# Delta heads of a decoder layer: the lower triangle made in mid-slot and stored whole, the decays one slot ahead

## The chip, the cores and the metric

The kernel runs on one core of a Trainium2 chip. The metric is the device time of one execution in microseconds; runs are compared by their medians. Engines are named PE or TensorE (matrix products), DVE or VectorE, ACT or ScalarE, POOL or GpSimd, and SP or SyncE, which here only issues DMAs.

## The reference

One decoder layer on x of shape (4, 512, 512), in float32: a gated delta rule with 16 heads of 128, then cross attention, then self attention and a mixture of experts. The change touches the delta heads only:

```python
q, k, v = conv_silu(x @ Wq.T), conv_silu(x @ Wk.T), conv_silu(x @ Wv.T)   # causal, 4 taps
g = exp(-exp(A_log) * softplus(a + dt_bias)); beta = sigmoid(b)
q, k = l2norm(q), l2norm(k)            # x / max(sqrt(sum x^2), 1e-12)
def step(S, (q_t, k_t, v_t, g_t, beta_t)):
    error = v_t - g_t * (S . k_t)
    S = g_t * S + k_t x (beta_t * error)
    return S, S . q_t
o = rmsnorm(o) * norm_w * silu(x @ Wg.T);  return o @ Wo.T
```

## The kernel before

**Chunks.** The recurrence is computed in chunks of 128 tokens, CH = 4 chunks (c = 0 to 3) in each of 16 heads, all four sequences of the batch at once (tiles of 128 x 4 x 128). Per chunk: `D` is the exponential of sums of log decays; `Lo` is the strictly lower triangle of k k^T times D and scales; the inverse of I + Lo (`W`, and `T` turned) gives `U` from `R` (v less what S retrieves); `PT` (q k^T times decays, turned) times U, plus `oi` (S times q), gives the output `o`; and S is updated with `Kd` and U.

**Slots.** `slot(i, c, ...)` is written out once for each engine, and each engine runs its list strictly in order; semaphores join the lists. The slot of chunk n merges the inverse and applies it for chunk n, makes q, v, the gate, P and Kd for chunk n+1, and k, the decays D and Lo for chunk n+2. The flags back, has1, has2 leave out what lies outside the range. The loop over heads holds the four slots of a head; the last head stands behind it.

**The inverse.** The sixteen-wide diagonal blocks of Lo (eight for each of four sequences) are inverted by GpSimd, on 32 partitions, in `solve`: a mask (L930), a diagonal (L932), 14 pairs of a product (L937) and a subtraction (L940), and a turned copy `W16` (L942). How they travel is SP's list: `diagonal_blocks` waits for `lo_ready` and stores the eight blocks with eight DMAs; `fetch_blocks` brings them to `L16` with 32 partitions; `spread` stores T16 and W16 into two zeroed images in DRAM and fetches the whole images as `T` and `W`. TensorE then merges blocks of 16 to 32, 64, 128: `spread_rows(l)` (W and Lo), `merge(l)` (Y and T), `turn_inverse(l)`; `spread_rows(0)` is a slot's first work and waits for `tw_in`.

**Order around the change.** In a slot of before, TensorE runs: spread_rows(0), half of k's projection, S k, merge(0), the other half, v turned, turn_inverse(0), spread_rows(1), q's projection around merge(1), turn_inverse(1), spread_rows(2), S q (for oi), v's projection around merge(2), the product for U, k k^T (kk), q turned, the products for o and S, the decay products (L635, L636), q k^T, k turned, the gate's projection, P turned, o turned. In c = 1 and c = 2 the raw weights of the next head are turned just ahead of the last step, and in c = 3 at two earlier places; ScalarE rounds them to `w_lead`, DVE makes `w_rest`. A projection is 12 products of 512 columns (L506). DVE's list has, late in the slot: the v taps, the squares of k (diag, its sum), o, S, P, Kd, then for both norms at once a maximum and a reciprocal of ScalarE's square root (L886), the scales `once` and `twice`, and Lo. GpSimd's list: Sd (S times a decay), in c = 2 and 3 a copy of a row of head constants, `lgm` (two products, the decay products' right side, L966), the solve, the halos of k, q and v (the last three tokens, carried to the next chunk), Dm (D cut to the triangle), grq and end, and the sum osq. A halo waits for ScalarE's copy of the projection (`copy_pre`, L820 and L821).

Of the kernel before, what the change touches and what calls it, by code (L numbers as in the profile page):

```python
# [5 lines left out]
ALU = mybir.AluOpType  # L6
# [6 lines left out]
P = 128  # L13
# [300 lines left out]
def delta_heads(nc, xn_parts, A, const_dram, ptab, osq, og_dram, blocks_dram, images_dram):  # L314
# [10 lines left out]
    with ExitStack() as ctx:  # L325
        sem = semaphores(nc, ctx, "gd")

        def sb(n, s, d=F32):
# [19 lines left out]
        root = sb("root", [P, 2, B])  # L348
        rn = sb("rn", [P, 2, 2, B])
# [25 lines left out]
        none = sb("none", [P, B, 4])  # L375
        L16 = sb("L16", [BK, SB, SB])
# [21 lines left out]
        kdiag, k_len, q_len, root_done, max_done, rnorm_done, once_ready, scales_done, extra_done = (  # L398
            sem(x) for x in ("kdiag", "klen", "qlen", "root", "max", "rnorm", "once", "scales", "extra"))
# [13 lines left out]
        def slots(eng, slot):  # L413

            slot(-1, 2, False, False, True, True)
            slot(-1, 3, False, True, True, True)
            with eng.Fori(0, LAST) as i:
                for c in range(CH):  # L420
                    slot(i, c, True, True, True, True)
            for c in range(CH):
                slot(LAST, c, True, c < CH - 1, c < CH - 2, False)

        @block.sync
        def _(sp):
# [4 lines left out]
            def diagonal_blocks(m, par):  # L431
                sp.wait_ge(lo_ready, m + 1)
                for k in range(P // SB):
                    rows = slice(k * SB, (k + 1) * SB)
                    sp.dma_start(blocks_dram[par, :, k].rearrange("b i j -> i b j"), Lo[rows, par, :, rows]).then_inc(lo_out, 16)

            def fetch_blocks(m, par, back):
                sp.wait_ge(lo_out, (m + 1) * 16 * (P // SB))
                if back:
                    sp.wait_ge(solved, m)  # L440
                sp.dma_start(L16[:].rearrange("p i j -> p (i j)"), blocks_dram[par].rearrange("b k i j -> (b k) (i j)")).then_inc(l16_in, 16)

            def spread(m, par):
                sp.wait_ge(solved, m + 1)
                for image, small in zip(images_dram, (T16, W16)):
# [4 lines left out]
                for image, whole in zip(images_dram, (T, W)):  # L450
# [7 lines left out]
            def slot(i, c, back, has1, has2, more):  # L458
# [3 lines left out]
                if has2:  # L462
                    diagonal_blocks(n + 2, c % 2)
# [28 lines left out]
        def _(pe):  # L492
# [31 lines left out]
            def slot(i, c, back, has1, has2, more):  # L524
# [63 lines left out]
                if back:  # L588
                    turn_inverse(1)
                    spread_rows(2)  # L590
# [22 lines left out]
                if has2:  # L613
                    pe.wait_ge(k_silu, n + 3)
                    if has1:
                        pe.wait_ge(lo_ready, n + 2)
                    each(Bk[4], k_c, k_c, kk_done)
                if has1:
# [3 lines left out]
                    turned(Bk[5], q_m, q_turned)  # L622
                if back:
# [7 lines left out]
                if has2:  # L631
                    pe.wait_ge(lgm_ready, n + 3)
                    if has1:
                        pe.wait_ge(d_exp, n + 2)
# [3 lines left out]
                if has1:  # L638
                    each(Bk[3], q_m, k_m, qk_done)
# [7 lines left out]
                if back and more and c in (1, 2):  # L647
                    pe.wait_ge(v_pre, n + 4)
                    turn_weights(i + 1, JK if c == 1 else JV)
                if back:  # L650
                    pe.wait_ge(o_ready, n + 2)
                    if has2:
                        pe.wait_ge(d_exp, n + 3)
# [11 lines left out]
        def _(dve):  # L665
# [14 lines left out]
            def slot(i, c, back, has1, has2, more):  # L680
# [45 lines left out]
                if back:  # L726
                    inverse_rows(1)
                    masked(2)
                if has1:
# [5 lines left out]
                if has1:  # L735
                    tap(n + 1, parm, PQ, cur_a, (2,), q_tap)
                    dve.wait_ge(v_halo, n + 2)
                    dve.wait_ge(v_pre, n + 4)
                    tap(n + 1, parm, PV, cur_a, (0, 1, 2), v_tap)
                if back and more and c == CH - 1:  # L740
                    rest_weights(h1, JG)
                if has2:
                    dve.wait_ge(kk_done, n + 3)
                    nc.vector.tensor_tensor(diag[:], Bk[4][:, :, :], ident.unsqueeze(1).to_broadcast([P, B, P]), ALU.mult).then_inc(kdiag, 1)
                    dve.wait_ge(kdiag, n + 3)
                    nc.vector.tensor_reduce(root[:, 0, :], diag[:], AX.X, ALU.add).then_inc(k_len, 1)
                if back:
                    dve.wait_ge(o_sum, n + 1)
                    dve.wait_ge(o2_ready, n + 1)
                    if c > 0:  # L750
                        for b in range(B):
                            st = nc.vector.scalar_tensor_tensor(out=o[:, b, :], in0=Bk[2][:, b, :], scalar=rn[:, par, 1, b:b + 1],
                                                                in1=oi[:, b, :], op0=ALU.mult, op1=ALU.add)
                        st.then_inc(o_ready, 1)
                    else:
                        nc.vector.tensor_tensor(o[:], Bk[2][:, :, :], bc(rn[:, par, 1, :], P), ALU.mult).then_inc(o_ready, 1)
                    dve.wait_ge(s_sum, n + 1)
                    if c > 0:
# [2043 lines left out]
```

## Time and profile before

| | us |
|---|---|
| median of 3 runs | 4028.65 |
| lowest, highest | 4025.49, 4032.96 |
| profiled execution, own time | 4027.95 |
| its span | 4026.1 |

| engine | busy us | share of the span |
|---|---|---|
| PE | 3447.7 | 86% |
| PE weight loads | 2733.0 | 68% |
| DVE | 2154.6 | 54% |
| ACT | 1774.1 | 44% |
| POOL | 1503.7 | 37% |

The page divides the span into 40 slices of 100 us. From the second to the twentieth PE is at nine tenths or more, and these are the delta heads (101 to some 1993 us); behind them come the other stages, which the change does not touch. A wait is read from the idle time just before an instruction, with what released it. Start times below are in microseconds from the start of the span. Matrix products of 128 by 128 in float32 stand twice for each product, so four sequences give x8.

### The profile page before, as it was taken

The numbers are of one execution on the slowest core, as the hardware profiler recorded it, in microseconds if no ns is written. First come the engines' busy times: TensorE is split into PE (matmuls) and PEld (weight loads), VectorE is DVE, ScalarE is ACT, GpSimd is POOL, SyncE is SP. The second block draws the span as 40 slices with busy tenths as digits, with TensorE's granted clock in tenths as the row PEclk, the third lists the DMA queues.
The fourth block names the chain that finished last, engine by engine and source line by source line (L and its number), as shares of the span: only waits on it lengthen the run. The fifth ranks groups of instructions, "written<-read, shape, count | busy, mean of one in ns | idle before, by whom it ended". The sixth has DMA issues, their size and how long they took to land. (4 is left out here: it accounts for less than half of the span.)

```text
span 4026.1 us, 62497 instructions
## 1 busy us (share of the span) xinstructions
PE 3447.7 (86%) x19682; PEld 2733.0 (68%) x19682; DVE 2154.6 (54%) x4501; ACT 1774.1 (44%) x4509; POOL 1503.7 (37%) x2924
## 2 busy tenths in 40 slices
PE   3799999999999999999799488869979999974993
PEld 1688888888888888888677244458856666654441
DVE  2566666666666666666432577745536546532223
ACT  2456555555655555556421155534434434431110
POOL 2466665656666666666300100045532000003203
PEclk9899999999999999999899699989989999985996
DMA  2111111111111111111243400023344120115324
GB/s 65 36 48 38 34 41 44 40 44 41 44 41 33 41 39 45 44 41 28 85 120 119 165 11 13 13 66 108 120 158 154 53 83 31 52 63 203 126 91 154
DMA packets 399009, 279.41 MB, mean 69 GB/s; under 512 B 137520, under 2 KB 323760, under 8 KB 397776
## 3 DMA queue, kind: packets, MB, share of 16 engines
q1 hardware_dynamic: 391504, 257.42, 21.2%
q0 software_dynamic: 5120, 16.78, 1.3%
q10 hardware_dynamic: 2304, 4.20, 0.3%
q8 instruction: 43, 0.70, 0.1%
q14 instruction: 38, 0.31, 0.0%
HBM read 179.22 MB, written 99.09 MB: 69 GB/s over the span
## 5 line engine op out<-in xcount | busy, mean ns | idle before, releaser
L506 PE MATMUL gd_PJ<-xn_lead,gd_w_rest 128*128 128x512 f32 x1024 | 449.6, 439 | 17.6 <-DVE gd_w_rest L669 17.6
L506 PE MATMUL gd_PJ<-xn_lead,gd_w_lead 128*128 128x512 f32 x1024 | 411.7, 402 | 0.0
L506 PE MATMUL gd_PJ<-xn_rest,gd_w_lead 128*128 128x512 f32 x1024 | 409.2, 400 | 0.0
L676 DVE SCALAR_TENSOR_TENSOR gd_conv<-gd_pre,gd_cur_a,gd_conv 128x512 f32<-128x512 f32 x384 | 298.1, 776 | 154.6 <-ACT gd_conv L821 147.5
L940 POOL TENSOR_TENSOR gd_T<-gd_T,gd_prod 32x14 f32<-32x14 f32 (+6 forms) x896 | 328.4, 366 | 70.2
L937 POOL TENSOR_TENSOR gd_prod<-gd_L,gd_T 32x14 f32<-32x14 f32 (+6 forms) x896 | 316.5, 353 | 70.2
L516 PE MATMUL gd_B<-gd_W,gd_Lo 128*128 128x64 f32 x1536 | 210.2, 283 | 95.5 <-DMA gd_W<-turned_image 95.5
L820 ACT COPY gd_pre<-gd_PJ 128x512 f32<-128x512 f32 x192 | 111.3, 580 | 380.3 <-PE gd_PJ L506 379.5
L516 PEld LDWEIGHTS gd_B<-gd_W,gd_Lo 128*128 128x128 f32 x1536 | 199.8, 203 | 103.3 <-DMA gd_W<-turned_image 89.7
L506 PEld LDWEIGHTS gd_PJ<-xn_lead,gd_w_rest 128*128 128x128 f32 x1024 | 199.0, 194 | 47.6 <-DVE gd_w_rest L669 21.8
L506 PEld LDWEIGHTS gd_PJ<-xn_lead,gd_w_lead 128*128 128x128 f32 x1024 | 197.3, 193 | 45.9
L506 PEld LDWEIGHTS gd_PJ<-xn_rest,gd_w_lead 128*128 128x128 f32 x1024 | 199.3, 195 | 27.0
L516 PEld LDWEIGHTS gd_B<-gd_Y,gd_T 128*128 128x128 f32 x1536 | 195.7, 192 | 25.6 <-DVE gd_Y L689 11.9
L2475 POOL MEMSET ms_rank<- 128x1 f32 x8 | 0.3, 98 | 561.4 <-POOLq L55 561.4
L2185 PE MATMUL sa_B<-sa_kT,sa_qT 128*128 128x512 f32 (+3 forms) x512 | 181.3, 478 | 29.7 <-DMA sa_qT<-turned_queries_keys 17.6
L695 DVE TENSOR_TENSOR gd_W<-gd_W,gd_B 128x256 f32<-128x256 f32 x192 | 80.6, 420 | 227.1 <-PE gd_B L516 227.0
L516 PE MATMUL gd_B<-gd_Y,gd_T 128*128 128x64 f32 x1536 | 195.7, 270 | 5.5 <-DVE gd_Y L689 5.5
L2249 ACT ACTIVATE sa_E<-sa_B,sa_nmax 128x512 f32<-128x512 f32 (+3 forms) x256 | 132.2, 524 | 152.4 <-DVE sa_nmax L2299 152.4
L2235 PE MATMUL sa_B<-sa_wo_lead,sa_o_parts 128*128 128x512 f32 x512 | 163.3, 400 | 8.8 <-issue 8.8
L1830 PE MATMUL sp_B<-sp_w_lead,sp_h_rest 128*128 128x512 f32 x384 | 157.6, 410 | 11.3 <-POOL sp_h_rest L1961 11.3
L1422 POOL TENSOR_TENSOR xt_xt<-x_xres,x_bpb 128x512 f32<-128x512 f32 x16 | 20.4, 1279 | 366.1 <-DVE xt_y L1638 305.3
L676 DVE SCALAR_TENSOR_TENSOR gd_conv<-gd_pre,gd_cur_k,gd_conv 128x512 f32<-128x512 f32 x192 | 153.4, 799 | 6.6 <-ACT gd_conv L821 4.3
(400 smaller groups left out, 8842.3 us busy)
## 6 DMA issues: line engine op xcount, KB each, us to landing
turned_queries_keys<-f_wq SPq DMA_DIRECT2D x16, 1280.0 KB, 6.0
gd_T<-inverse_image SPq DMA_DIRECT2D x64, 256.0 KB, 2.9
gd_W<-turned_image SPq DMA_DIRECT2D x64, 256.0 KB, 3.3
gated_outputs<-gd_og SPq DMA_DIRECT2D x64, 256.0 KB, 2.6
go_ogt<-gated_outputs SPq DMA_DIRECT2D x16, 1024.0 KB, 6.8
sa_qT<-turned_queries_keys SPq DMA_DIRECT2D x16, 1024.0 KB, 5.6
gathered<-sa_blank SPq DMA_DIRECT2D x39, 256.0 KB, 7.2
ms_xr<-gathered SPq DMA_DIRECT2D x39, 256.0 KB, 2.7
```

The costliest lines, as they stand in the source:

```text
L506: mm = pe.matmul(bank, w_parts[wp][:, j, k, :], rhs, start=(k == 0 and wp == 1), stop=(k == KT - 1 and wp + xp == 0))
L516: mm = pe.matmul(bank[:, b, :], lhs[b], rhs[b], start=True, stop=True)
L676: nc.vector.scalar_tensor_tensor(out=conv[:, j], in0=pre[:, parm, j, :, d:d + P], scalar=cur[:, 4 * j + d:4 * j + d + 1], in1=conv[:, j], ...
L695: nc.vector.tensor_tensor(second(W_c, s), second(W_c, s), half[3].rearrange("p b (g m) -> p b g m", m=s), ALU.add).then_inc(w_ready, 1)
L820: nc.scalar.copy(pre[:, parm, j, :, 3:3 + P], bank)
L937: nc.gpsimd.tensor_tensor(prod[:, rows, 0:j], L16[:, rows, j:j + 1].to_broadcast(shape), T16[:, j:j + 1, 0:j].to_broadcast(shape), ALU.mul ...
L940: nc.gpsimd.tensor_tensor(T16[:, rows, 0:j], T16[:, rows, 0:j], prod[:, rows, 0:j], ALU.subtract).then_inc(solving, 1)
L1422: nc.gpsimd.tensor_tensor(xt[:, par, :], xres[:, bass.ds(t, 1), :].rearrange("p o d -> p (o d)"), bpb[:, :], ALU.add).then_inc(bias_ready, 1)
L1830: mm = pe.matmul(bank[:, :], h_parts[hp][:, s, k, :], w_parts[wp][:, k, j, :], start=(k == 0 and hp == 1), stop=(k == KT - 1 and hp + wp = ...
L2185: pe.matmul(Bk[bank][:, col:col + w], qT[:, h, i * P:(i + 1) * P], kT[:, h // REP, 0:w], start=True, stop=False)
L2235: mm = pe.matmul(Bk[i][:, :], part(o_parts, h, op)[:, i * P:(i + 1) * P], wo_parts[wp][:, h, :], start=(h == 0 and op == 1), stop=(h == HE ...
L2249: ex = nc.scalar.activation(E[:, par, E_AT[i]:E_AT[i] + w], Bk[bank][:, col:col + w], ACT.Exp, bias=nmax[:, par, i:i + 1], accum_out=sums[ ...
```

## The change

- **Lo in mid-slot.** TensorE computes kk ahead of spread_rows(2). DVE forms the diagonal's product ahead of masked(2) and its sum (`kss`) behind it. ScalarE takes the square root of kss alone (`klen`), behind the oi copies and ahead of q's SiLU. DVE then makes the maximum, the reciprocal (`krn`), once, twice and Lo between q's last tap and the v taps.
- **q's norm.** ScalarE sums q's squares into `qss`; DVE takes the maximum with 1e-24; GpSimd raises it to -0.5 (`qrn`), ahead of grq.
- **Whole triangle stored once.** SP stores all of Lo (256 KB) with one DMA, and fetch_blocks picks the diagonal blocks out of DRAM with a stride. In spread, W goes ahead of T.
- **Decays one slot ahead.** A further flag has3: lgm, the decay products, Exp and Dm's source belong to chunk n+3. lgm now reads the table `ptab`, and stands on GpSimd behind the halos. A slot (-1, 1) is added at the start.
- **Others.** q k^T stands behind q's turning, ahead of the product for o. On ScalarE, U is copied ahead of v's projection. In c = 1 and 2 the raw weights are turned ahead of the decay products, rounded ahead of Exp, and w_rest stands behind S. GpSimd's solve stands first in its slot, with the row copy behind its first instruction, and Sd behind it.

ScalarE, slot c = 1, from the oi copies to the square of q; before:

```order
L854 ACTIVATE gd_oi<-gd_B1,gd_grq 128x128 x4
L825 ACTIVATE gd_qT<-gd_conv 128x512
L820 COPY gd_pre<-gd_PJ 128x4x128
L821 ACTIVATE gd_conv<-gd_PJ,gd_cur_a 128x512
L863 COPY gd_U<-gd_B1 128x512
L870 ACTIVATE gd_osqr,gd_root<-gd_B5 128x128 x4
```

And in the changed kernel:

```order
L867 ACTIVATE gd_oi<-gd_B1,gd_grq 128x128 x4
L871 ACT_TABLE_LOAD
L871 ACTIVATE gd_klen<-gd_kss 128x4
L838 ACT_TABLE_LOAD
L838 ACTIVATE gd_qT<-gd_conv 128x512
L877 COPY gd_U<-gd_B1 128x512
L833 COPY gd_pre<-gd_PJ 128x4x128
L834 ACTIVATE gd_conv<-gd_PJ,gd_cur_a 128x512
L888 ACTIVATE gd_osqr,gd_qss<-gd_B5 128x128 x4
```

The square root with two table loads has come between the oi copies and q's SiLU, and U's copy stands ahead of v's.

TensorE, slot c = 1, from the product for U to k's turning; before (B4 holds kk, B3 q k^T, B0 the decay sums):

```order
L516 MATMUL gd_B1<-gd_R,gd_W 128x128 x4
L516 MATMUL gd_B4<-gd_kT 128x128 x4
L521 MATMUL gd_B5<-gd_cst,gd_qT 128x128 x4
L516 MATMUL gd_B2<-gd_U,gd_PT 128x128 x4
L516 MATMUL gd_B1<-gd_U,gd_Kd 128x128 x4
L635 MATMUL gd_B0<-gd_lgm_rest,gd_upr 128x512
L636 MATMUL gd_B0<-gd_lgm_lead,gd_upr 128x512
L516 MATMUL gd_B3<-gd_kT,gd_qT 128x128 x4
L521 MATMUL gd_B5<-gd_cst,gd_kT 128x128 x4
```

And in the changed kernel, the same place:

```order
L521 MATMUL gd_B1<-gd_R,gd_W 128x128 x4
L526 MATMUL gd_B5<-gd_cst,gd_qT 128x128 x4
L521 MATMUL gd_B3<-gd_kT,gd_qT 128x128 x4
L521 MATMUL gd_B2<-gd_U,gd_PT 128x128 x4
L521 MATMUL gd_B1<-gd_U,gd_Kd 128x128 x4
L641 REGISTER_ALU
L502 MATMUL gd_PJ<-gd_cst,gd_wraw 128x128 x4
L647 MATMUL gd_B0<-gd_lgm_rest,gd_upr 128x512
L648 MATMUL gd_B0<-gd_lgm_lead,gd_upr 128x512
```

kk has left this place (it stands ahead of spread_rows(2)), q k^T has moved up, and the weights are turned ahead of the decay products.

GpSimd, from the end of one slot to the solve of the next (osq to T16), before:

```order
L991 TENSOR_TENSOR osq<-osq,gd_o2 128x4
L957 TENSOR_TENSOR gd_Sd<-gd_S,gd_end 128x512
L966 TENSOR_TENSOR gd_lgm_lead<-gd_cur_k,gd_cst 128x512
L966 TENSOR_TENSOR gd_lgm_rest<-gd_cur_k,gd_cst 128x512
L927 ISA
L929 REGISTER_ALU
L930 TENSOR_TENSOR gd_T16<-gd_L16,gd_below 32x256
```

And in the changed kernel, from the solve's last instruction in c = 1 to the end of the slot:

```order
L952 TENSOR_TENSOR gd_W16<-gd_T16,gd_blank 32x256
L977 TENSOR_TENSOR gd_Sd<-gd_S,gd_end 128x512
...
L992 TENSOR_TENSOR gd_lgm_lead<-ptab,gd_cst 128x512
...
L992 TENSOR_TENSOR gd_lgm_rest<-ptab,gd_cst 128x512
L998 TENSOR_TENSOR gd_Dm<-gd_D,gd_tril 128x512
L1001 TENSOR_TENSOR gd_qrn<-gd_qss,gd_minus_half 128x4
L1003 TENSOR_TENSOR gd_grq<-gd_cur_a,gd_qrn 128x4
L1004 COPY gd_end<-gd_cur_a 128x4
L1008 TENSOR_TENSOR osq<-osq,gd_o2 128x4
```

Sd and lgm have gone from ahead of the solve to behind it.

The diff, cut to its core:

```diff
-            def diagonal_blocks(m, par):
+            def store_triangle(m, par):
                 sp.wait_ge(lo_ready, m + 1)
-                for k in range(P // SB):
-                    rows = slice(k * SB, (k + 1) * SB)
-                    sp.dma_start(blocks_dram[par, :, k].rearrange("b i j -> i b j"), Lo[rows, par, :, rows]).then_inc(lo_out, 16)
+                sp.dma_start(lo_dram[par, :, 0:P, :].rearrange("b t s -> t b s"), Lo[:, par]).then_inc(lo_out, 16)
 ...
+                a = lo_dram[par]
+                src = bass.AP(tensor=a.tensor, offset=a.offset, ap=[[SB * P + SB, BK], [P, SB], [1, SB]])
+                sp.dma_start(L16[:], src).then_inc(l16_in, 16)
 ...
                     turn_inverse(1)
+                if has2:
+                    pe.wait_ge(k_silu, n + 3)
+                    if has1:
+                        pe.wait_ge(lo_ready, n + 2)
+                    each(Bk[4], k_c, k_c, kk_done)
+                if back:
                     spread_rows(2)
 ...
                     turned(Bk[5], q_m, q_turned)
+                    if back:
+                        pe.wait_ge(pt_ready, n + 1)
+                    each(Bk[3], q_m, k_m, qk_done)
 ...
+                if has3:
+                    pe.wait_ge(lgm_ready, n + 4)
+                    if has2:
+                        pe.wait_ge(d_exp, n + 3)
 ...
+                if has2:
+                    act.wait_ge(k_len, n + 3)
+                    nc.scalar.activation(klen[:, :], kss[:, :], ACT.Sqrt).then_inc(k_root, 1)
                 if has1:
                     act.wait_ge(q_tap, (n + 2) * 3)
                     silu(PQ, qT[:, parm, :], q_silu)
-                    act.wait_ge(v_proj, n + 2)
-                    copy_pre(parm, PV, JV, cur_a, v_pre)
 ...
                     pool.wait_ge(v_pre, n + 4)
+                    if has2:
+                        pool.wait_ge(darg, n + 3)
                     halo(parm, c1, PV, v_halo)
+                if has3:
+                    for part, col in zip(lgm, (P_LG, P_LGR)):
+                        at = col + c3 * B
+                        lg = ptab[:, bass.ds(h3, 1), at:at + B].rearrange("p o n -> p (o n)")
+                        tt = nc.gpsimd.tensor_tensor(part[:], bc(lg, P), later.unsqueeze(1).to_broadcast([P, B, P]), ALU.mult)
+                    tt.then_inc(lgm_ready, 1)
 ...
+                    pool.wait_ge(q_max, n + 2)
+                    nc.gpsimd.tensor_tensor(qrn[:, parm, :], qss[:, :], minus_half[:], ALU.pow).then_inc(q_rnorm, 1)
```

## Rows read from the trace of the kernel before

**Rows 1.** Busy time by stage, 14 heads: length, PE, PEld, DVE, ACT, POOL, clock, DMA.
```profile
293.37:1917.67 1624.30, 1526.62 (x10192) 1372.12 (x10192) 1019.31 (x2142) 919.83 (x2296) 1012.29 (x2311) 0.97 0.16 40
```

**Rows 2.** Waits of PE, 200 to 1800 us: total us, times, longest.
```profile
PE gd_B L516 <- DMA gd_W<-turned_image: 69.7, 28, 4.5
```

**Rows 3.** PE in order of time, starts of slots: start, us, instruction, [idle before <-releaser].
```profile
1018.99 1.00 PE L516 MATMUL gd_B<-gd_W,gd_Lo 128*128 128x64 f32 x8
1020.77 0.50 PE L506 MATMUL gd_PJ<-xn_lead,gd_w_rest 128*128 128x512 f32 x1 [0.78 <-DVE gd_w_rest L669]
...
1022.27 1.05 PE L516 MATMUL gd_B<-gd_S,gd_kT 128*128 128x128 f32 x8
...
1047.77 1.10 PE L516 MATMUL gd_B<-gd_W,gd_Lo 128*128 128x64 f32 x8 [1.00 <-DMA gd_W<-turned_image]
...
1105.42 1.97 PE L516 MATMUL gd_B<-gd_W,gd_Lo 128*128 128x64 f32 x8 [3.92 <-DMA gd_W<-turned_image]
...
1109.86 1.73 PE L516 MATMUL gd_B<-gd_S,gd_kT 128*128 128x128 f32 x8
```

**Rows 4.** Busy time in a stretch behind the long wait; the clock is third from last.
```profile
1106.00:1108.00 2.00, 2.00 (x9) 1.90 (x9) 0.42 (x1) 0.00 (x0) 0.77 (x1) 0.50 0.07 6
```

**Rows 5.** SP and POOL in order of time: slots c=1 (first two rows) and c=2.
```profile
993.68 0.72 POOL L930 TENSOR_TENSOR gd_T<-gd_L,gd_below 32x256 f32<-32x256 f32 x1 [3.00 <-DMA gd_L<-diagonal_blocks]
...
1006.75 0.84 POOL L942 TENSOR_TENSOR gd_W<-gd_T,gd_blank 32x256 f32<-32x256 f32 x1
...
1019.17 3.60 SPq L435 DMA_DIRECT2D diagonal_blocks<-gd_Lo  x8
...
1021.30 0.20 POOL L991 TENSOR_TENSOR osq<-osq,gd_o 128x4 f32<-128x4 f32 x1 [3.34 <-ACT gd_osqr L898]
...
1025.61 0.72 POOL L930 TENSOR_TENSOR gd_T<-gd_L,gd_below 32x256 f32<-32x256 f32 x1 [0.66 <-DMA gd_L<-diagonal_blocks]
...
1040.73 0.84 POOL L942 TENSOR_TENSOR gd_W<-gd_T,gd_blank 32x256 f32<-32x256 f32 x1
...
1044.28 0.51 SPq L451 DMA_DIRECT2D gd_W<-turned_image  x1
```

**Rows 6.** PE in order of time, middle of slot c=1.
```profile
1003.68 1.00 PE L516 MATMUL gd_B<-gd_W,gd_Lo 128*128 128x64 f32 x8
1004.52 1.11 PE L516 MATMUL gd_B<-gd_S,gd_qT 128*128 128x128 f32 x8
...
1009.15 1.05 PE L516 MATMUL gd_B<-gd_R,gd_W 128*128 128x128 f32 x8
...
1010.93 0.60 PE L521 MATMUL gd_B<-gd_cst,gd_qT 128*128 128x128 f32 x4
...
1013.07 0.48 PE L635 MATMUL gd_B<-gd_lgm_rest,gd_upr 128*128 128x512 f32 x1
```

**Rows 7.** ACT in order of time, middle of slot c=1.
```profile
1003.12 0.64 ACT L825 ACTIVATE gd_kT<-gd_conv 128x512 f32<-128x512 f32 x1 [2.81 <-DVE gd_conv L676]
...
1005.67 1.14 ACT L854 ACTIVATE gd_oi<-gd_B,gd_grq 128x128 f32<-128x128 f32 x4 [0.76 <-PE gd_B L516]
1008.34 0.63 ACT L825 ACTIVATE gd_qT<-gd_conv 128x512 f32<-128x512 f32 x1 [1.53 <-DVE gd_conv L676]
1009.35 0.59 ACT L820 COPY gd_pre<-gd_PJ 128x512 f32<-128x512 f32 x1 [0.37 <-PE gd_PJ L506]
1009.83 0.78 ACT L821 ACTIVATE gd_conv<-gd_PJ,gd_cur_a 128x512 f32<-128x512 f32 x1
```

**Rows 8.** ACT, the table loads around the square root in slot c=1.
```profile
1015.62 1.28 ACT L886 ACT_TABLE_LOAD   x1
1016.91 0.21 ACT L886 ACTIVATE gd_root<-gd_root 128x8 f32<-128x8 f32 x1
1017.14 1.28 ACT L889 ACT_TABLE_LOAD   x1
```

**Rows 9.** Groups of POOL instructions, whole run: busy us, mean ns, idle before.
```profile
L966 POOL TENSOR_TENSOR gd_lgm_rest<-gd_cur_k,gd_cst 128x512 fp32r<-128x512 f32 x64 | 66.5, 1040 | 0.0
```

More of the change, by code:

```diff
@@ L522, in turned, with slot @@
                 tr.then_inc(done, 1)
-            def slot(i, c, back, has1, has2, more):
+            def slot(i, c, back, has1, has2, has3, more):
                 n = i * CH + c
@@ L678, in tap, with slot @@
                                                    op0=ALU.mult, op1=ALU.add).then_inc(done, 1)
-            def slot(i, c, back, has1, has2, more):
+            def slot(i, c, back, has1, has2, has3, more):
                 n = i * CH + c
@@ L736, in slot @@
                     tap(n + 1, parm, PQ, cur_a, (2,), q_tap)
[L737 to L741, printed above, removed]
-                if has2:
[L743 to L758, printed above, removed]
-                        dve.wait_ge(sd_ready, i * (CH - 1) + c)
-                        nc.vector.tensor_tensor(S[:], Bk[1][:, :, :], Sd[:], ALU.add).then_inc(s_ready, 1)
-                    else:
-                        nc.vector.tensor_copy(S[:], Bk[1][:, :, :]).then_inc(s_ready, 1)
@@ L825, in silu, with slot @@
                 nc.scalar.activation(dst, conv[:, j].rearrange("p b t -> p (b t)"), ACT.Silu).then_inc(done, 1)
-            def slot(i, c, back, has1, has2, more):
+            def slot(i, c, back, has1, has2, has3, more):
                 n = i * CH + c
@@ L891, in slot @@
                     nc.scalar.copy(PT[:], Bk[3][:, :, :]).then_inc(pt_ready, 1)
-                if back and more and c in (1, 2):
-                    lead_weights(i + 1, JK if c == 1 else JV)
                 if back:
@@ L942, in solve, with slot @@
                 nc.gpsimd.tensor_tensor(W16[:], T16[:].rearrange("p i j -> p j i"), blank[:], ALU.add).then_inc(solved, 1)
-            def slot(i, c, back, has1, has2, more):
+            def slot(i, c, back, has1, has2, has3, more):
                 n = i * CH + c
@@ L957, in slot @@
                     nc.gpsimd.tensor_tensor(Sd[:], S[:], bc(end[:, par, :], P), ALU.mult).then_inc(sd_ready, 1)
-                if has1 and c == CH - 1:
-                    row(cur_a, h1, head_a)
-                if has2:
-                    if c == 2:
-                        row(cur_k, h2, head_k)
-                    if has1:
-                        pool.wait_ge(darg, n + 2)
-                    for part, col in zip(lgm, (P_LG, P_LGR)):
-                        tt = nc.gpsimd.tensor_tensor(part[:], bc(cur_k[:, col + c2 * B:col + c2 * B + B], P),
-                                                     later.unsqueeze(1).to_broadcast([P, B, P]), ALU.mult)
-                    tt.then_inc(lgm_ready, 1)
-                if has1:
-                    solve(n + 1, back)
                 if has2:
```

179 lines of the change are left out of this document (107 added, 72 removed).

## The prediction

> **What bounds the kernel now.** I read in this order: busy time by stage, what TensorE waits for, one head in order of time, then the chain behind the longest wait. In the steady part of the delta stage TensorE is busy 1526.62 of 1624.30 us, at a mean granted clock of 0.97 [rows 1]. No other engine comes near, so the stage lasts as long as TensorE's work, plus its idle time, plus what a lowered clock costs. The idle time has one large cause: the first products of a slot, which need W and T from their images in DRAM. Fourteen heads hold 28 such waits, 69.7 us in all [rows 2], two in each head of four slots. In the head shown they are 1.00 us at 1047.77 (start of slot c=3) and 3.92 us at 1105.42 (start of c=1) [rows 3]. [...] From the slot's first products to those of S and k it is 4.44 us (1105.42 to 1109.86); after a start at full clock it is 3.28 with 0.78 of waiting in it (1018.99 to 1022.27), so 2.50. The products of S and k then take 1.73 instead of 1.05 [rows 3]. That is 1.94 + 0.68 = 2.6 us per head. The third item is the 0.78 us for w_rest at 1020.77 [rows 3].
>
> **Why the images are late.** In slot c=2 Lo is stored from 1019.17 by eight DMAs that take 3.60 us to issue; GpSimd, free since 1021.50, does its other work and begins the solve when the blocks have landed, at 1025.61; W16 is done at 1041.57, the last image fetch is issued at 1044.28, and TensorE starts at 1047.77 [rows 3, 5]. From the start of the solve to TensorE's start it is 22.2 us, in a slot of 28.8.
>
> **What the change takes away.** Lo no longer comes at the end of DVE's slot but in its middle, so it is stored, fetched and waiting before the next slot begins. Now GpSimd's own end of slot starts the solve: the osq addition, over at 1021.50, against 1025.61, 4.1 us earlier [rows 5]. The 2.1 us of lgm and 1.04 of Sd stand behind the solve. The solve may get shorter too: it took 13.9 us in c=1 (993.68 to 1007.59) and 15.96 in c=2 (1025.61 to 1041.57) [rows 5]. DVE's v taps begin when ScalarE has scaled v, 1010.61 in c=1 [rows 7], 8.4 before the next slot and after the solve; the same point of c=2 is 1038.4, inside it. Started earlier, the solve ends ahead of the v taps in every slot. The chain of 22.2 us from 2.5 us after the slot's start gives images at about 24.7 at the latest, against a slot of 26.5 to 28. So I take both waits as gone: 31 of them (28, and 3 more outside the window read) at 69.7 / 28 = 2.49 is 77 us; the clock with them, 15 x 2.6 = 39; and 15 of the 0.78 waits, 12, since the raw weights are now turned ahead of the decay products and rounded ahead of Exp. **Removed: 128 us.** The store grows from eight pieces of 4 KB to one of 256 KB; the nearest rows are the image fetches of that size, of which TensorE saw the last landed 3.5 us after issue (1044.28 to 1047.77) [rows 3, 5]. Before, Lo was stored 2.05 us after the root's end (1017.12 to 1019.17) [rows 5, 8]; with the root ending at 3.8 on the scale below, Lo is ready at about 5.9, over 8 us before the slot's end at 14.5, so this is covered.
>
> **What it puts in the way.** Time zero is the start of the S and q products, 1004.52, in slot c=1; the PE and ScalarE rows of that slot give the rest [rows 6, 7].
> - *The key products (kk)* now stand ahead of the products at 1003.68. They need kT, whose SiLU ends at 1003.76. So TensorE waits where it did not: 0.15 to 0.2 us in each of some 62 slots, **12 us**. Their own 0.89 us (half of 1009.15 to 1010.93) is only moved.
> - *The square root in mid-slot.* ScalarE's oi copies end at 2.29. Then a table load of 1.28, the root 0.21, a table load of 1.28 [rows 8], and qT's SiLU of 0.63: done at 5.75, against 4.45 before. TensorE reaches the turning of q at 5.52 (u products at 4.63 plus 0.89), where it had kk as cover before. It waits 0.3 us. In the 47 slots with c > 0: **14 us**. (In c = 0 there is no oi, the loads run early and nothing waits.)
> - *The decays one slot ahead.* lgm now stands on GpSimd behind the halo of v, which waits for v's projection on ScalarE. ScalarE: qT to 5.75, U (a copy of 0.59) to 6.25 with the usual overlap, v's copy and scaling (1009.35 to 1010.61, 1.26) to 7.4 [rows 7]. GpSimd: halo 0.2 (as the osq addition [rows 5]), two lgm products of 1.04 [rows 9]: ready at 9.7 to 9.8. TensorE: q turned at 5.8, then the turning, o and s products (1010.93 to 1013.07, 2.14) and the moved query-key products, 0.89, to 8.83, a weight turning of 0.36 (2.14 less two times 0.89), 9.2 [rows 6]. It waits 0.5 us. Before, lgm was made at the slot's start and nothing waited for it. In c = 0, u to v ready is 1.06 + 0.59 + 1.16 = 2.8, lgm at 5.1 after u's start, while TensorE is there at 0.89 + 2.14 + 0.89 = 3.9: 1.2 us. Sum 47 x 0.5 + 15 x 1.2 = **42 us**.
>
> The two small edits have one answer: the two square roots that were one become a ScalarE root for k and a power on GpSimd for q, off the path, since the power comes some 2 us ahead of the osq addition for which GpSimd waits anyway; no row shows a power, and the nearest, additions on 128x4 such as osq's, take 0.20 [rows 5]. Moving the query-key products earlier gives U's copy its cover back and costs nothing.
>
> **Sum.** New waits 12 + 14 + 42 = 68; 128 - 68 = 60. Filling and draining the pipeline has the same chain twice (eight stores become one, 3.60 us of issue [rows 5]); I take 5 us. The profiled execution took 4027.95 us (span 4026.1), near the median of 4028.65. **Forecast: 4027.95 - 65 = 3963 us.** Bounds of each unknown: the new waits are 0 at least (every one sits on 0.2 to 1.2 us of estimated edge) and could be 110 if each chain is 0.7 us slower than put together here, since they add up directly: 3895 to 4005.
>
> [...] The rows say that a switch of table costs its 1.28 us and nothing else: the root at 1016.91 follows the load begun at 1015.62 by 0.01 us, and the next load begins 0.02 after the root ends (1016.91 + 0.21 to 1017.14) [rows 8]. [...]
>
> **Rivals.**
> - *The new waits hardly show.* TensorE arrives later than I reckon, or the chains overlap more; then only the removal counts with a third of the new waits: 4027.95 - 128 + 22 - 5 = 3917, at the extreme 3895. For it: all three new waits are small against the rows they come from. Against: each follows from rows of one slot, and the slots repeat. Chance 0.17.
> - *The images stay late.* The changed blocks fetch and the whole-triangle store are not in the rows; if the blocks land after GpSimd is free, the solve starts no earlier. If half of the 77 + 39 us stays, 4027.95 - 128 + 58 + 68 - 5 = 4021, with new waits then partly hidden behind the stall, about 4005. Against it: Lo is ready some 8 us before the slot's end and needs about 3.5 + 3.5. Chance 0.10.
> - *ScalarE's mid-slot chain becomes the bound: slower.* The chain oi, root, qT, U, v, halo, lgm has no slack in my sum, so each microsecond more costs one per slot, 62 us. It decides from 65 / 62 = 1.05 us: beyond that the kernel is slower. [...] For it: three engines hand over in turn, and I count each hand-over as next to nothing. Against it: the rows with loads show no such gap. Chance 0.07. [...]
> - *GpSimd becomes the bound.* Solve, Sd, halos and lgm now stand in one line ahead of TensorE's decay products. From 2.5 after the slot's start: solve 14.5, Sd 1.04, halos and a row copy 0.8, so free at about 19. Zero above is 14.5 us before the next slot's first products (1004.52 to 1018.99) [rows 3, 6], so about 13.3 into a slot of 27.8, and v is ready at 13.3 + 7.4, nearly 21: 2 us of slack. A solve that stays at 16 still fits; a power that overruns all slack by 3 us would give 3963 + 3 x 62 = 4149. Chance 0.04, and 0.04 more for a small overrun that ends within 0.2%.
>
> **How the numbers follow.** Forecast case, 3935 to 3995: 0.58. The rivals have 0.17, 0.10, 0.07 and 0.08. The range takes in the forecast case, most of the first two rivals and the bounds above: 3900 to 4010. A difference of 0.2% (8 us) is about what can be told from none. Faster: 0.58 + 0.17 + most of the second rival, 0.84; within 0.2%: 0.06; slower: 0.10.
>
> **What would show it.** Right: no wait of TensorE for W's image in the steady slots; a mean clock of 0.99 or 1.00 there; the osq addition directly ahead of the solve; waits of TensorE for lgm of about 0.5 us (1.2 in c = 0), for qT about 0.3, for kT about 0.2; a table load of 1.28 after the oi copies; heads of about 112 us instead of 116. Wrong: image waits that remain; a wait of GpSimd for the blocks ahead of the solve; waits for lgm that end with GpSimd's products long after v is ready (GpSimd late), or waits for qT over 1 us (the chain on ScalarE).

## The result and the profile after

The changed kernel takes 4043.32 us (median of 6 runs, 4039.44 to 4045.72), the kernel before 4029.52 (median of 6): a ratio of 1.0035, 95% interval 1.0022 to 1.0048. The forecast of 3963 us and its range of 3900 to 4010 were wrong, and so was the sign. The profiled execution of after has a span of 4037.6 us.

A head of four slots is read off the copies of gd_cur_a on GpSimd, one per head: before 116.02 us on the mean of 14 heads, after 117.69 ((1889.77 - 242.11) / 14). The steady stretch of after, beside [rows 1], and all waits of TensorE from 200 to 1800 us, beside [rows 2]:

```profile
299.63:1942.95 1643.32, 1538.27 (x10195) 1359.79 (x10193) 1165.99 (x2198) 985.31 (x2351) 1076.33 (x2366) 0.98 0.18 48
```
```profile
PE gd_B L647 <- POOL gd_lgm_rest L992: 90.9, 55, 3.5
PE gd_PJ L511 <- DVE gd_w_rest L677: 5.7, 14, 0.4
PE gd_B L526 <- ACT gd_qT L838: 4.1, 26, 0.2
PE gd_B L521 <- ACT gd_kT L838: 0.3, 1, 0.3
```

The image waits (69.7 us there) are gone, and 90.9 us of waiting for the decay products lgm stand in their place; the clock rose only from 0.97 to 0.98. DVE is busy for 1165.99 us in 14 heads instead of 1019.31, with almost the same work (2198 instructions instead of 2142, the 56 more of them small). In order of time, one slot with c > 0 (c = 1), the three engines around that wait:

```profile
1026.96 0.22 POOL L931 TENSOR_TENSOR gd_pre<-gd_pre,gd_none 128x12 f32<-128x12 f32 x1 [3.97 <-ACT gd_conv L834]
1027.13 1.49 POOL L992 TENSOR_TENSOR gd_lgm_lead<-ptab,gd_cst 128x512 fp32r<-128x512 f32 x1
1028.58 1.49 POOL L992 TENSOR_TENSOR gd_lgm_rest<-ptab,gd_cst 128x512 fp32r<-128x512 f32 x1
```
```profile
1026.92 3.70 DVE L684 SCALAR_TENSOR_TENSOR gd_conv<-gd_pre,gd_cur_a,gd_conv 128x512 f32<-128x512 f32 x3 [0.52 <-ACT gd_conv L834]
```
```profile
1028.43 0.60 PE L502 MATMUL gd_PJ<-gd_cst,gd_wraw 128*128 128x128 f32 x4
1030.12 0.50 PE L647 MATMUL gd_B<-gd_lgm_rest,gd_upr 128*128 128x512 f32 x1 [1.09 <-POOL gd_lgm_rest L992]
```

v's scaled copy releases GpSimd's halo and DVE's three v taps at the same moment. They run side by side and both are slow: a product takes 1.49 us instead of 1.04 [rows 9], the three taps 3.70. TensorE waits 1.1 us, in c = 1, 2 and 3. In c = 0 it waits 3.50, and the cause lies earlier:

```profile
1095.71 0.20 POOL L1008 TENSOR_TENSOR osq<-osq,gd_o 128x4 f32<-128x4 f32 x1 [1.80 <-ACT gd_osqr L909]
1099.48 0.72 POOL L937 TENSOR_TENSOR gd_T<-gd_L,gd_below 32x256 f32<-32x256 f32 x1 [3.57 <-issue]
...
1115.06 1.03 POOL L992 TENSOR_TENSOR gd_lgm_lead<-ptab,gd_cst 128x512 fp32r<-128x512 f32 x1
1116.06 1.03 POOL L992 TENSOR_TENSOR gd_lgm_rest<-ptab,gd_cst 128x512 fp32r<-128x512 f32 x1
```
```profile
1117.14 0.71 PE L647 MATMUL gd_B<-gd_lgm_rest,gd_upr 128*128 128x512 f32 x1 [3.50 <-POOL gd_lgm_rest L992]
```
```profile
1118.00:1120.00 2.00, 2.00 (x8) 1.73 (x7) 2.00 (x4) 1.07 (x2) 0.32 (x1) 0.50 0.92 269
```

GpSimd has nothing to wait for ("issue") and still stands for 3.57 us at the first instruction of its loop body, in each of the 14 turns back to the loop's start (3.3 to 4.2 us). The last head stands behind the loop and has no such gap: its solve starts 0.02 us after osq, its wait for lgm in c = 0 is 1.92 us and the slot takes 26.9 instead of 30.1 to 31.2. In the loop the solve and everything behind it come that much later, and the clock behind TensorE's stall is 0.50, as it was behind the image wait [rows 4]. DVE is caught too: its v taps now begin while GpSimd is still at the late solve, and the last of the three takes 4.95 us instead of 0.75 (6.53 for the three), in the same 14 turns:

```profile
1112.35 6.53 DVE L684 SCALAR_TENSOR_TENSOR gd_conv<-gd_pre,gd_cur_a,gd_conv 128x512 f32<-128x512 f32 x3 [0.85 <-ACT gd_conv L834]
```

It ends at 1118.88, 0.55 us after GpSimd's row of W16, three halos, lgm and Dm (1113.25 to 1118.33). TensorE does not wait for it there, being late itself.

The page has one more hint, the queue for instructions (packets, MB, share), before and after:

```profile
q14 instruction: 38, 0.31, 0.0%
```
```profile
q14 instruction: 108, 0.88, 0.1%
```

Seventy more packets of 8 KB are five for each of the 14 times that the loop goes back to its start. GpSimd's compiled program of after has 67072 bytes for 1048 instructions, 64 bytes each, so a packet of 8192 bytes holds 128. The loop is instructions 159 to 493 from the start of that program (the trace leaves out the first 26). In the trace the five packets of a turn begin when GpSimd has come to numbers 160, 164 to 166, 225 to 229, 353 and 476.

### The profile page after: what moved, and what is told of

It reads as the page before. It is cut to its first block and busy times, and to the rows that moved or that the text cites. A ratio compares the mean times of both kernels' runs of the same rounds, so it can differ in the third digit from the quotient of the medians.

```text
span 4037.6 us, 62353 instructions
## 1 busy us (share of the span) xinstructions
PE 3452.8 (86%) x19651; PEld 2714.7 (67%) x19682; DVE 2312.6 (57%) x4563; ACT 1845.2 (46%) x4568; POOL 1580.2 (39%) x2989
## 5 line engine op out<-in xcount | busy, mean ns | idle before, releaser
L684 DVE SCALAR_TENSOR_TENSOR gd_conv<-gd_pre,gd_cur_a,gd_conv 128x512 f32<-128x512 f32 x384 | 457.3, 1191 | 46.2 <-ACT gd_conv L834 39.3
L950 POOL TENSOR_TENSOR gd_T<-gd_T,gd_prod 32x14 f32<-32x14 f32 (+6 forms) x896 | 305.9, 341 | 70.2
L947 POOL TENSOR_TENSOR gd_prod<-gd_L,gd_T 32x14 f32<-32x14 f32 (+6 forms) x896 | 278.7, 311 | 70.7
L521 PE MATMUL gd_B<-gd_W,gd_Lo 128*128 128x64 f32 x1536 | 192.6, 268 | 0.0
L521 PEld LDWEIGHTS gd_B<-gd_W,gd_Lo 128*128 128x128 f32 x1536 | 186.7, 192 | 0.0
```

The costliest lines, as they stand in the source:

```text
L521: mm = pe.matmul(bank[:, b, :], lhs[b], rhs[b], start=True, stop=True)
L684: nc.vector.scalar_tensor_tensor(out=conv[:, j], in0=pre[:, parm, j, :, d:d + P], scalar=cur[:, 4 * j + d:4 * j + d + 1], in1=conv[:, j], ...
L947: nc.gpsimd.tensor_tensor(prod[:, rows, 0:j], L16[:, rows, j:j + 1].to_broadcast(shape), T16[:, j:j + 1, 0:j].to_broadcast(shape), ALU.mul ...
L950: nc.gpsimd.tensor_tensor(T16[:, rows, 0:j], T16[:, rows, 0:j], prod[:, rows, 0:j], ALU.subtract).then_inc(solving, 1)
```

## The experiments

Theory A: lgm is late because of its place. Theory B: GpSimd fetches its own code again in every head. "Head" is measured as above.

| kernel | median us | ratio to before, interval | head | code packets |
|---|---|---|---|---|
| e1_lgm_first | 4035.11 | 1.0022, 1.0012 to 1.0032 | 117.38 | 108 |
| e2_short | 4047.03 | 1.0047, 1.0031 to 1.0064 | 117.77 | 38 |
| e3_first_short | 3953.44 | 0.9817, 0.9800 to 0.9833 | 111.31 | 38 |
| e4_before_padded | 4029.61 | 1.0001, 0.9992 to 1.0011 | 116.09 | 108 |
| e5_after_shifted | 4013.20 | 0.9964, 0.9950 to 0.9978 | 115.29 | 39 |
| e6_first_shifted | 3955.59 | 0.9813, 0.9797 to 0.9830 | 111.73 | 39 |
| e7_short_misplaced | 4032.37 | 1.0005, 0.9994 to 1.0015 | 117.07 | 109 |
| e8_pm_early | 3945.00 | 0.9788, 0.9772 to 0.9804 | 110.98 | 38 |
| e9_decay_first | 3918.08 | 0.9729, 0.9714 to 0.9743 | 109.31 | 38 |
| e10_squares_first | 3915.80 | 0.9714, 0.9700 to 0.9728 | 108.80 | 38 |
| e11_between_halos | 4109.06 | 1.0194, 1.0173 to 1.0214 | 121.76 | 39 |

### The products first: e1_lgm_first

```diff
+                if has3:
+                    if has2:
+                        pool.wait_ge(darg, n + 3)
+                    for part, col in zip(lgm, (P_LG, P_LGR)):
...
                     start_solve(n + 1, back)
...
                     pool.wait_ge(v_pre, n + 4)
-                    if has2:
-                        pool.wait_ge(darg, n + 3)
                     halo(parm, c1, PV, v_halo)
-                if has3:
-                    for part, col in zip(lgm, (P_LG, P_LGR)):
```

> The changed kernel with one move: on GpSimd the two decay products (lgm) and their wait for the last decay argument stand at the head of the slot, ahead of the first instruction of the solve, where before they stood behind the v halo. Two theories on the new loss. Theory A (place): the products come late because they stand behind the v halo, and each takes 1.49 us because DVE's v taps run beside them. It expects the TensorE wait for lgm_rest gone in c = 1, 2, 3 (1.09 to 1.11 us each now), the products near 1.04 us, three v taps back from 3.70 to near 2.4 us. Theory B (code): the 3.57 us in which GpSimd sits at the top of every head with nothing to wait for is its own code being loaded again; this kernel's loop is as long, so B expects that gap to stay near 3.5 us, but no longer in front of lgm: it then delays the solve of c = 0 by 3.5 + 2.1 us, and the images of the next slot come some 2 to 3 us late. With both: heads of 117.2 - 3 x 1.1 - 3.5 - 1 (half clock) + 3 = 112 to 113 us, time 3965 to 3985 us. With A alone and no gap: 109.5 us a head, 3925 us. If the place doesn't matter: 4040 us.

The lgm waits are gone and a product takes 1.04 us, as A says. Of the taps A is right in c = 0 alone, where three take 2.39 us; in c = 1 and c = 2 they take 3.28 and 3.76, now beside Dm, where they took 3.70. The gap stays, 45.7 us in 14 heads, as B says, and now delays the whole solve of c = 0. TensorE's next slot:

```profile
1114.31 0.63 PE L526 MATMUL gd_B<-gd_cst,gd_o 128*128 128x128 f32 x4 [1.89 <-ACT gd_D L899]
1116.61 1.10 PE L521 MATMUL gd_B<-gd_W,gd_Lo 128*128 128x64 f32 x8 [1.68 <-DMA gd_T<-inverse_image]
```
```profile
1118.00:1120.00 2.00, 2.00 (x6) 1.56 (x5) 0.18 (x1) 0.00 (x0) 2.00 (x3) 0.50 0.62 146
```

The place was worth 8 us only (forecast 60 to 80). The late images and the half clock are back: with the wait in front of it that slot (c = 1) is 31.0 to 32.8 us long here, against 28.6 in after. And where nothing is late on GpSimd, the 1.1 us of waiting for lgm were mostly cover for something else: in c = 2 TensorE now waits 0.90 us for Pm (the masked query-key product on DVE), in c = 3 1.25 for ScalarE's squares of q, and these slots are only 0.25 and 0.17 us shorter.

### A shorter loop: e2_short and e3_first_short

```diff
-                    halo(parm, c1, PQ, q_halo)
                     pool.wait_ge(v_pre, n + 4)
-                    halo(parm, c1, PV, v_halo)
+                    halo(parm, c1, PQ, v_halo)
...
-                        tt = nc.gpsimd.tensor_tensor(part[:], bc(lg, P), later.unsqueeze(1).to_broadcast([P, B, P]), ALU.mult)
+                    nc.gpsimd.tensor_tensor(lgm_both[:], two.unsqueeze(3).to_broadcast(whole),
+                                            later.unsqueeze(1).unsqueeze(1).to_broadcast(whole), ALU.mult).then_inc(lgm_ready, 1)
```

> The changed kernel with its order kept and GpSimd's loop body made shorter: the q and v halos are one instruction (behind q's and v's pre), and the two decay products are one instruction over both tables (128x1024 where there were two of 128x512). GpSimd's program then has 15 instructions less in the loop of four slots, about as many as the kernel before the change has. Theory B (GpSimd's loop does not fit what it holds of its code and is fetched again in every head): the 3.57 us gap at the top of the head goes to about 0.2 us, the instruction packets of the small queue go from 108 back to about 40, lgm is waited for about 1.1 us in c = 0 as in the other slots instead of 3.5 us, and the half clock behind it goes: 15 x (2.4 + 1.0) = 51 us less, 3985 to 3995 us. Rival C (the gap is the four weight loads, which SP now issues at that moment, or anything else of the order): nothing changes, 4035 to 4045 us with the gap in place. In c = 1, 2, 3 both expect the wait for lgm to stay at 1.1 us, since place and overlap are the same.

> Both edits: the decay product at the head of GpSimd's slot, and the short loop body. If A and B are both right no TensorE wait for lgm is left, no gap and no late image: 15 x (4 x 1.1 + 2.4 + 1.0) = 117 us less than the changed kernel, 3920 to 3935 us, heads of 109.4 us, clock 0.99 to 1.00. If only A holds (the gap stays): as the kernel with the move alone. If only B holds: as the kernel with the short body alone.

With the short loop the packets are 38, the gap is 4.2 us in 13 heads instead of 46.8, and c = 0 takes 27.1 us instead of 30.1 to 31.2. But the time doesn't fall. Theory B had 3985 to 3995 us; rival C had about the time that came, but with the gap still in place, and the gap is gone. Slots c = 1 and c = 2 grew from 28.6 to 29.4: TensorE's wait for lgm is half as long (0.55), but one product of 1024 beside the v taps stretches these from 3.70 to 4.83 us, and Pm, which stands behind them on DVE, is 1.15 late. Slot c = 3 grew most, from 29.9 to 31.1 and in every second head 32.7: behind the same taps the rest of the gate weights is 1.0 late, and in those heads the clock is 0.50 behind that wait. So e2 confirms B for c = 0 and hides it by a change of its own, which is why e5 below takes the reload away in another way. With both edits it is 3953 us: no wait for lgm, a gap of 0.4 us, no image wait; the head is 6.4 us shorter, though either edit alone gave nothing (0.3 and -0.1). That is 90 us of the 117 expected. What is left are waits that the sum of the expectation did not have, for Pm (19.5 us from 200 to 1800) and for the squares of q (17.4).

### Length or place of the loop: e4, e5, e6, e7

Each adds only increments of an unused semaphore to GpSimd's program: 24 inside the loop of the kernel before (e4), 100 ahead of the loop (e5: of after; e6: of e1), 36 ahead of it (e7: of e3).

```diff
             pool.wait_ge(masks_set, 2 * SB - 1)
+            for _ in range(100):
+                pool.sem_inc(padding, 1)
```

> The kernel before the change, with nothing added but six increments of an unused semaphore in each slot of GpSimd's loop, placed ahead of its last wait of the slot, where it idles 2 to 3 us: 24 more instructions in the loop of four slots, so that the loop ends where the changed kernel's does. They cost some 0.3 us of GpSimd's idle time. Theory B: GpSimd's code is now fetched again in every head here too: instruction packets of the small queue from 38 to about 100, a gap of about 3.5 us with nothing to wait for at the first instruction of c = 0 (0.24 us now), and since solve and decay products start late there, later images or decays in that slot: 15 x 2 to 4 = 30 to 60 us slower, 4060 to 4090 us. Rival C (length is not the cause): gap 0.2 us, 38 packets, 4025 to 4035 us.

> The changed kernel with 100 increments of an unused semaphore ahead of GpSimd's loop (at the start, where GpSimd waits for constants); the loop itself is the same, instruction for instruction, and only lies 100 instructions further on in GpSimd's program: it spans numbers 259 to 593 instead of 159 to 493, and code is fetched in blocks of 8 KB, which are 128 instructions. The runs so far have a reload in every head where the loop ends at number 488, 493 or 496 and none where it ends at 472 or 476; lengths are 331 and more against 324 and less. Theory L (the length of the loop decides): nothing changes, 108 packets, gap 3.5 us, 4038 to 4046 us. Theory P (its place decides: the end comes too near to the next 8 KB boundary, which here is 47 instructions away): 38 packets, gap 0.2 to 0.4 us; c = 0 then takes 25.3 + 1.1 + about 0.6 = 27 us as in the kernel with the short body instead of 30 to 31, c = 1, 2, 3 stay at 28.6, 28.6, 29.9: 114.1 us a head, 15 x 3.3 = 50 less, 3985 to 4000 us.

> The kernel with the decay products at the head of GpSimd's slot (4035 us) and the same 100 increments ahead of the loop, which then spans numbers 258 to 588. Theory P: no reload; the gap of 3.3 us ahead of the products goes, and with it the waits that it had become in c = 1 (1.9 to 2.1 us for the decays, 1.0 to 1.7 us for the image, and the half clock behind them): slots of 25.5, 27.9, 28.2, 29.75 us as in the kernel with both edits, 111.3 us a head instead of 117.4, 3945 to 3958 us. Theory L: 4028 to 4040 us, as without the shift.

> The kernel with both edits (decay products first, short loop body, 3953 us), and 36 increments of an unused semaphore ahead of GpSimd's loop: 319 instructions in the loop as before, at numbers 190 to 508 instead of 154 to 472, so its end lies 4 instructions ahead of an 8 KB boundary. Theory P: the reload comes back though the loop is short: about 108 packets, a gap of 2.5 to 3.5 us at the head of c = 0, late decays and images in c = 1, 4025 to 4040 us. Theory L: 38 packets, 3950 to 3957 us.

GpSimd's waits for "issue" at the head of the loop, 200 to 1800 us, in before, e4, e5 and e7:

```profile
POOL gd_lgm_lead L966 <- issue: 3.4, 14, 0.3
```
```profile
POOL gd_lgm_lead L967 <- issue: 35.7, 14, 2.8
```
```profile
POOL gd_T L938 <- issue: 4.7, 14, 0.4
```
```profile
POOL gd_lgm_both L972 <- issue: 47.4, 14, 3.7
```

The same loop without a reload when it lies 100 instructions on (e5, e6), and the short loop with one when it lies 36 on (e7): its place decides, not its length. In after, e1, e4 and e7 the last three packets of a turn begin at 222 to 229, 350 to 353 and 476 to 482, that is 27 to 36 instructions ahead of 256, 384 and 512, multiples of the 128 instructions of a packet. Counted in such blocks of 8 KB from the start of the compiled program, the reload came where the loop's last instruction lies 4, 16, 19 or 24 ahead of a boundary (e7, e4, after, e1) and not where it lies 36, 40, 40, 47 or 52 ahead (e2, e3, before, e5, e6). That the distance to a boundary is what counts rests on this fit alone. Where the edge lies between 24 and 36, and why there, was not measured.

In e4 the gap is 2.5 us in every head and the time is the same, because the solve waited for its blocks anyway: GpSimd's waits for them fell from 92.3 us to 61.9, and TensorE's for the images are 72.0 us instead of 69.7. The change, which brings the blocks early, took that cover away. In e5 the time falls by 30 us, not by 50: TensorE still waits 1.9 us for lgm in c = 0, and behind that the clock is 0.50 in 11 of 14 heads (28.5 us instead of 26.9 where it is not). e6 has neither cause and comes out as e3 does, at 3956. Its waits of TensorE are for other things:

```profile
PE gd_B L527 <- DVE gd_Pm L800: 25.0, 43, 0.9
PE gd_B L527 <- ACT gd_osqr L889: 17.5, 14, 1.3
```

### Between the halos: e11_between_halos

```diff
                     halo(parm, c1, PQ, q_halo)
+                if has3:
+                    if has2:
+                        pool.wait_ge(darg, n + 3)
+                    for part, col in zip(lgm, (P_LG, P_LGR)):
...
                     pool.wait_ge(v_pre, n + 4)
                     halo(parm, c1, PV, v_halo)
```

> The shifted kernel (4013 us: no reload, order of the changed kernel), and one move on GpSimd: the two decay products stand between the q halo and the wait for v's pre, in the 1.4 to 4.0 us in which GpSimd idles, instead of behind the v halo. It tells whether it is the v halo's wait alone that makes them late, or whether they must stand at the slot's head. By the rows of the shifted kernel the q halo ends 4.0 us ahead of v's pre in c = 1, so both products of 1.04 us are done ahead of the v taps, and 1.5 to 1.6 us ahead in c = 0 and c = 2, so there the second runs into the taps by some 0.5 us. Expected where the wait alone decides: the waits for lgm_rest (1.09 us, and 1.91 in c = 0 with the half clock behind it) gone or under 0.3 us, taps 2.4 to 3.3 us, 15 x 3.7 = 56 less: 3955 to 3965 us. If GpSimd's line is too full there: 3980 us and more, with lgm waits of 0.5 us and over left in c = 0 and c = 2.

The waits for lgm are gone, and it is 96 us slower than e5, which neither expectation had. GpSimd's idle time was not free time for DVE:

```profile
960.78 5.27 DVE L763 TENSOR_TENSOR gd_once<-gd_cur_k,gd_krn 128x8 f32<-128x8 f32 x1
966.09 0.17 DVE L765 TENSOR_TENSOR gd_twice<-gd_once,gd_krn 128x8 f32<-128x8 f32 x1
```
```profile
960.44 0.87 POOL L953 TENSOR_TENSOR gd_W<-gd_T,gd_blank 32x256 f32<-32x256 f32 x1
961.28 1.03 POOL L978 TENSOR_TENSOR gd_Sd<-gd_S,gd_end 128x512 f32<-128x512 f32 x1
962.27 0.20 POOL L932 TENSOR_TENSOR gd_pre<-gd_pre,gd_none 128x12 f32<-128x12 f32 x1
962.45 0.20 POOL L930 TENSOR_TENSOR gd_pre<-gd_none 128x12 f32<-128x12 f32 x1
962.61 1.03 POOL L991 TENSOR_TENSOR gd_lgm_lead<-ptab,gd_cst 128x512 fp32r<-128x512 f32 x1
963.61 1.03 POOL L991 TENSOR_TENSOR gd_lgm_rest<-ptab,gd_cst 128x512 fp32r<-128x512 f32 x1
964.60 0.20 POOL L930 TENSOR_TENSOR gd_pre<-gd_none 128x12 f32<-128x12 f32 x1
964.77 1.25 POOL L1000 TENSOR_TENSOR gd_Dm<-gd_D,gd_tril 128x512 f32<-128x512 f32 x1
```

A product on 128x8, 0.17 us elsewhere, began 0.34 us after GpSimd began W16 and ended at 966.05, within 0.03 us of the end of GpSimd's unbroken row of eight instructions (964.77 + 1.25). With the products in it, that row became long enough to hold DVE for a fifth of a slot. Over 200 to 1800 us this one group of DVE takes 2.12 us on the mean instead of 0.18 in e6; TensorE's waits move to Pm (67.5 us), to W in the merge (22.2) and to qT (13.3), and the clock falls to 0.50 behind most waits of 2.0 to 2.8 us. Here, and in c = 0 of after, DVE stood still across a whole row of GpSimd instructions; but in c = 1 of after the two took turns, one tap (1.41 us) and one product (1.49) at a time. What decides between the two was not measured. At the slot's head (e1, e3, e6) DVE mostly idles: in e3 and e6 all DVE instructions that overlap the products are together 0.9 us longer than the shortest of their kind (280 to 1900 us), against 117 us in after.

### What is late next: e8, e9, e10

e8 starts from e3 and moves Pm on DVE from behind the rest of a weight to directly behind o. e9 adds a move on ScalarE, e10 one more there:

```diff
-                    act.wait_ge(v_tap, (n + 2) * 3)
-                    silu(PV, vT[:, :], v_silu)
...
                     nc.scalar.activation(D[:], Bk[0][:, :, :], ACT.Exp).then_inc(d_exp, 1)
+                if has1:
+                    act.wait_ge(v_tap, (n + 2) * 3)
+                    silu(PV, vT[:, :], v_silu)
```
```diff
-                if back and more and c == CH - 1:
-                    lead_weights(h1, JG)
...
                     sq.then_inc(q_len, 1)
+                if back and more and c == CH - 1:
+                    lead_weights(h1, JG)
```

> The kernel with both edits (3953 us) and one more move, on DVE: the masked query-key product Pm stands directly behind o, ahead of the new state S and of a weight's rest, instead of behind them. TensorE waits for Pm 0.20 us in c = 0, 0.44 in c = 1 and 0.69 in c = 2 there. Theory D (with the decays on time, the next to end last is DVE's line behind the v taps, in the order in which its results are wanted): Pm comes 0.6 to 1.2 us earlier, these waits go, S still lands ahead of its product of the next slot (2.3 us into it), 15 x 1.3 = 20 us less: 3930 to 3940 us. Rival: S or the weight's rest is late in its place, 3950 to 3960 us.

> The kernel with Pm early (3945 us), and on ScalarE the decays' exponential (with its wait for the decay argument) ahead of the v silu instead of behind it. At the slot's end TensorE waits for that exponential 0.28, 0.52 and 0.62 us in three of four slots there. It stands behind the v silu, which waits for DVE's v taps, and behind a table load of 1.28 us. Theory D2 (the wait is the load put behind the taps): the load now falls into the 2.35 us in which ScalarE idles for the taps, the exponential ends some 0.9 us earlier, the three waits go: 15 x 1.4 = 21 us less, 3920 to 3930 us. Rival: the v silu and the gate then stand behind the second load, and o or P waits for them instead: 3940 to 3950 us.

> The kernel of the run before it, and in c = 3 alone ScalarE takes the squares of q ahead of the rounded copy of the gate weights. TensorE waits 1.24 us in every c = 3 for these squares (it turns k into the bank they read). Two theories: the wait goes, 15 x 1.2 = 18 us less, 3902 to 3912 us; or the rest of the gate weights, which DVE can take only behind that copy and ahead of o, becomes the next to end last at the same place (0.3 to 0.8 us of the 1.2 stay): 3908 to 3920 us.

e8: the waits for Pm are gone (1.33 us per head), those for D rose from 0.21 to 1.4; the head fell by 0.33 us and the time by 8 from e3 to e8, not by 20. e9 took those away: 27 us. In e10 the wait for the squares (1.25) is gone, and the rest of the gate weights is late in its place, 0.94 to 0.97: the rival expected. The 2 us between e9 and e10 are within the scatter of their runs; the head is 0.5 us shorter. At 3915.8 us e10 is 115 us under the kernel before beside it (4030.42); its clock is 1.00 from 200 to 1800 us.

## Why the prediction failed, step by step

- **Removed, 128 us (image waits, half clock, w_rest): the mechanism was right.** The image waits are gone, osq stands directly ahead of the solve in c > 0, and the images come early: their last fetch is issued 6 to 11 us ahead of the slot's first products and lands 3.3 us later (median). In c = 0 the solve's start, said to follow osq, came 3.57 us after it.
- **kk, 12 us, and the square root in mid-slot, 14 us: right.** The weight loads for kT and qT waited 11.1 and 14.2 us from 200 to 1800 us in after. (The list of the products themselves has only 4.4 of this: it drops short gaps, and the ends of products are modelled.) The load, root, load of c = 1 took 1.28, 0.20 and 1.28 us with 0.02 between them. The rival of ScalarE's chain fell.
- **lgm, 42 us: the failed term.** It measured about 100 us, and some 27 more of half clock behind it. Its clocking up to v was exact: 7.4 us after the start of the S and q products was said, 1026.88 - 1019.45 = 7.4 measured. Then two products of 1.04 were counted and took 1.49, beside DVE's taps. Ready after 10.6 instead of 9.7 to 9.8: 1.09 us instead of 0.5 in each slot with c > 0. In c = 0 it is 3.50 instead of 1.2, because GpSimd's line was taken to begin with osq; without the gap, in the last head, it is 1.92. Together 90.9 us for 55 waits, or about 100 for all 62, and the clock behind the long wait was not in the sum at all. By an estimate from slot lengths it costs 1.2 to 2.4 us per head (slot c = 0 is 30.1 to 31.2 us, 3.5 of it waiting, against 25.4 in e6 without its own wait), some 27 us for 15 heads.
- **The sum again:** new waits 12 + 14 + 100 + 27 = 153 against 128 removed: 25 slower, and 23.4 is what fourteen heads show. The time rose by 14 and the span of the profiled executions by 11.5: up to the second row copy it takes 4.0 us more (242.1 instead of 238.1), from the last row copy to TensorE's last product of the delta heads 10.5 less (118.5 instead of 129.0), in the stages behind 5.5 less. Filling did not get shorter, though the forecast said so; the end did, and it holds the last head, which has no image waits and no reload.
- **The rival "GpSimd becomes the bound"** (0.04 + 0.04) is the nearest to what happened, but its price came from the solve and the power. The power takes 1.02 us, not 0.20, and is off the path as said. What used up its 2 us of slack in c = 0 was the 3.57 us of code, for which no row of before had a sign.
- **How much each cause weighs.** Without reload and with lgm at the head the same change gives 3955.6 us, 0.2% from the forecast of 3963, so with both causes gone nearly the whole miss is gone. That it comes so near is luck: the forecast had 42 us of waits for lgm, of which e6 has none, and e6 has 42.5 us (in 14 heads) of waits for Pm and for the squares of q, which the forecast did not have. Most of the difference is slot c = 0, 30.5 us on the mean of 13 heads in after and 25.7 in e6; the three others together are only 1.1 us shorter. The causes don't add: against after, the place alone gives 8 us, the reload alone 30, both 88. Each left a stall in c = 0 or c = 1 long enough for the half clock behind it.

## What to carry to other kernels

Count a moved GpSimd operation twice: at its duration, and as time in which a DVE instruction beside it may stand still (5.27 us for one of 0.17 in e11), and put it where DVE idles, not where GpSimd does. After any change of GpSimd's loop, compare the code packets and the idle time at the loop's first instruction; idle instructions ahead of the loop were worth 30 us (e5) and 80 (e6) here. When a fix of a late engine gives nothing, look at what was late behind it before dropping it: here two fixes gave 8 and 30 us, and 88 together. And when a wait is to go, ask which engine comes next: 1.1 us of waiting for lgm in c = 2 and 3 was worth 0.2 to 0.3 us, because Pm and the squares of q were nearly as late.

## What the runs showed of the hardware

- A loop on GpSimd was fetched again in every turn (five packets of 8 KB, and 2.5 to 3.6 us on the mean of standing still at its first instruction) where its end lay 4 to 24 instructions ahead of an 8 KB boundary of its program (after, e1, e4, e7: ends at number 488 to 508), and not where it lay 36 to 52 ahead (before, e2, e3, e5, e6: 472, 476, 588, 593). A packet of 8192 bytes holds 128 of GpSimd's instructions, of 64 bytes each.
- A DVE instruction that begins beside GpSimd's work can last until GpSimd's unbroken row ends: 5.27 us for a 128x8 product of 0.17 (e11), 4.95 for a tap of 0.75 (c = 0 of after, in all 14 heads). It can also get its turn between two of them: 1.41 us for a tap (c = 1 of after).
- A wait of TensorE of 3.50 us was followed by a granted clock of 0.50 in every head of after, one of 1.90 in 11 of 14 heads of e5, single waits of 1.1 us (after, c > 0) and 1.25 (e3, c = 3) never. In c = 3 of e2 three short waits close together (0.53, 0.46, 1.0) were, in 7 of 14 heads.
- Two table loads in mid-slot took 1.28 us each, with gaps of 0.02 us around the root between them.
- Raising 128x4 numbers to a power takes GpSimd 1.02 us, where an addition of that size takes 0.20.
